# Seven block products for the third chunk's gate and up, with the pair's operand sums moved ahead, in an fp32 feed-forward kernel

## What is computed

```python
# first layer; every sequence b has its own low-rank matrices (rank 16), F = 1376
gate = x @ W_gate.T + 0.5 * lora(x, A_gate[b], B_gate[b])
up   = x @ W_up.T   + 0.5 * lora(x, A_up[b], B_up[b])
act  = silu(gate) * up
down = act @ W_down.T + 0.5 * lora(act, A_down[b], B_down[b])
x = x + down @ sign(W_ffn).T + bias0
# second layer
y = lora(x, B1[b], A1[b])
x = x + y @ (W1 + 2 * sum_n w_n * lora_B_n @ lora_A_n).T + bias1
```

## Time and profile before

| | us |
|---|---|
| median of 3 runs | 877.64 |
| lowest, highest | 876.82, 879.19 |
| the profiled execution | 876.61 |
| its span | 874.8 |

### The profile page before, as it was taken

One profiled execution on the slowest core, in us unless ns is written; L12 is line 12 of the kernel. 1 busy time (PEld: TensorE's weight loads), 2 busy tenths in 40 slices (PEclk: granted clock), 3 DMA queues, 4 the chain that ended last, 5 costly groups with the idle time before them and its releaser, 6 DMA issues.

```text
span 874.8 us, 21938 instructions
## 1 busy us (share of the span) xinstructions
PE 868.2 (99%) x7474; PEld 714.5 (82%) x7474; DVE 523.5 (60%) x1204; ACT 230.8 (26%) x460; POOL 86.5 (10%) x122
## 2 busy tenths in 40 slices
PE   9999999999999999999999999999999999999998
PEld 6888888888888888888888888888888888888885
DVE  5797555656555565656556655655656565556644
ACT  4953221222222122222212222212123122212210
POOL 0232000000000000000000000000000000000011
PEclk9999999999999999999999999999999999999999
DMA  9957777575777767577776757677775757777653
GB/s 338 415 218 251 237 232 249 188 242 156 235 248 227 244 209 238 156 234 231 236 236 226 241 166 233 195 248 239 230 243 176 235 175 243 246 226 247 204 133 94
DMA packets 161819, 197.22 MB, mean 225 GB/s; under 512 B 58112, under 2 KB 127744, under 8 KB 154112
## 3 DMA queue, kind: packets, MB, share of 16 engines
q1 hardware_dynamic: 103584, 108.76, 40.4%
q10 hardware_dynamic: 56096, 80.76, 27.3%
q0 software_dynamic: 2112, 7.34, 2.1%
HBM read 150.37 MB, written 15.20 MB: 189 GB/s over the span
## 4 chain that ended last, share of the span: by engine, by line
PE 95%; SPq 2%; DMA 1%; DVE 1%; issue 0%; ACT 0%; ACTq 0%; DVEq 0%
PE gu_ps L1132 54%; PE y_ps L1237 26%; PE out_ps L1259 3%; PE gu_ps L1346 2%; PE out_ps L1310 2%; PE gu_ps L1337 1%; PE y_ps L1132 1%; PE out_ps L1246 1%; PE out_ps L1132 1%; PE gu_ps L1237 1%; PE out_ps L1267 1%; DMA rows_sb<-in_btab 1%; SPq L352 0%; SPq L444 0%; DMA la_raw<-in_la 0%
## 5 line engine op out<-in xcount | busy, mean ns | idle before, releaser
L1237 PE MATMUL y_ps<-down_sb,actT_sb 128*128 128x512 f32 x1023 | 246.9, 394 | 0.0
L1237 PEld LDWEIGHTS y_ps<-down_sb,actT_sb 128*128 128x128 f32 x1023 | 189.7, 188 | 58.7 <-issue 21.4
L1132 PE MATMUL gu_ps<-wg_sb,xT_sb 128*128 128x432 f32 x768 | 163.8, 362 | 0.5 <-DVE act_all L842 0.5
L1132 PE MATMUL gu_ps<-wu_sb,xT_sb 128*128 128x432 f32 x768 | 160.7, 358 | 0.0
L1132 PEld LDWEIGHTS gu_ps<-wg_sb,xT_sb 128*128 128x128 f32 x768 | 141.7, 188 | 11.6 <-DVE xT_sb L824 1.4
L1132 PEld LDWEIGHTS gu_ps<-wu_sb,xT_sb 128*128 128x128 f32 x768 | 144.4, 188 | 8.0
L544 POOL TENSOR_TENSOR b_two<-b_raw,const_sb 128x128 f32<-128x128 f32 x62 | 23.5, 400 | 630.2 <-DMA b_raw<-in_b1tab 630.2
L598 ACT CAST actT_sb<-landed 128x512 fp32r<-128x512 f32 (+1 forms) x96 | 50.5, 584 | 127.1 <-issue 76.7
L610 ACT ACTIVATE act_all<-gu_ps 128x432 f32<-128x432 f32 (+1 forms) x96 | 49.6, 551 | 88.6 <-PE gu_ps L1337 83.6
L1132 PE MATMUL gu_ps<-slot,s_sb 128*128 128x512 f32 x270 | 66.8, 392 | 0.0
L846 DVE STREAM_TRANSPOSE act_all<-act_all 128x512 f32<-128x512 f32 (+1 forms) x96 | 64.0, 667 | 3.3
(11 more groups left out here) (173 smaller groups left out, 911.6 us busy)
## 6 DMA issues: line engine op xcount, KB each, us to landing
slot<-t_table ACTq DMA_DIRECT2D x59, 1024.0 KB, 7.7
a_raw<-in_atab SPq DMA_DIRECT2D x128, 152.0 KB, 7.5
rows_sb<-in_btab SPq DMA_DIRECT2D x128, 118.0 KB
landed<-act_all SPq DMA_DIRECT2D x132, 64.0 KB, 2.5
xT_raw<-in_xT SPq DMA_DIRECT2D x32, 256.0 KB, 6.3
x_in<-in_x SPq DMA_DIRECT2D x32, 256.0 KB, 8.1
landed<-act_all ACTq DMA_DIRECT2D x124, 64.0 KB, 2.7
out_x<-out_sb SPq DMA_DIRECT2D x31, 256.0 KB, 5.2
```

The costliest lines, as they stand in the source:

```text
L1132: last = nc.tensor.matmul(o, w, m, start=start and n == 0, stop=stop and n == len(terms) - 1, skip_group_check=not check)
L1237: last = nc.tensor.matmul(to[:], actT_sb[:, ACTT_SLOT[c] + n, a, :], down_sb[:, blk, b, :], start=begin and (c, n) == (0, 0) and (a, b) == ...
```

## The change

Chunk 2 gets the same seven block products (q1 to q7) as chunk 1. Its weights leave wg_sb and wu_sb and are kept as four blocks v11, v21, v12, v22; its differences of weights are made by GpSimd in the opening and stored unsplit in vt_table; in the loop ScalarE loads them (432 KB each, four times a pair) into vslot0 and vslot1, and they are split there each time (high_side_t, low_side_t). The products of a step are ordered anew, chunk 0 last. first_sums, low_s and high_s of the next pair go ahead of add_out, silu and gating in an odd step. x1_turn lies over x_in; the last step's x has a tile of its own. In the odd steps, send_act of chunk 1 and ScalarE's half of send_x1 move into the next even step. The core of the diff:

```diff
@@ SP, before step 0
+            sp.dma_start(vt_raw[1][:], wside[:, half(0)]).then_inc(S["vraw_in"], 16)
...
@@ GpSimd
             t_store(1, S["first_out"])
+            pool.wait_ge(S["vraw_in"], 4 * 16)
+            side_difference(1, 3, 1)
...
+            for n in range(1, 5):
+                pool.dma_start(vt_table[n - 1], vt_raw[n][:].rearrange("p k w -> p (k w)")).then_inc(S["vt_out"], 16)
             t_store(2, S["first_out"])
@@ ScalarE, step
                 if parity == 0 and seven(j):
-                    copy_p1(g, j)
+                    copy_p1(j)
+                    copy_q1(j)
+                    send_act(act, prev, 1)
+                    high_s(4, j)
+                    load_side_t(3)
+                    send_x1(act, pp, range(0, 2))
+                if isinstance(g, int) and g == 1:
+                    act.wait_ge(S["vt_out"], 4 * 16)
...
                 copy_lhs(g)
                 if parity == 0 and seven(j):
+                    load_t(3, L["slot0_in"])
                     load_t(4, L["slot1_in"])
-                    load_t(3, L["slot0_in"])
+                    high_side_t(3, j)
+                    high_side_t(4, j)
                 if parity == 1 and nxt is not None:
...
+                    load_side_t(1)
+                    load_side_t(2)
                     load_t(1, L["slot0_in"])
                     if seven(j):
                         load_t(2, L["slot1_in"])
...
+                if parity == 1 and nxt is not None:
+                    high_s(1, j + 1)
+                    high_s(2, j + 1)
+                for c in range(NC):
+                    silu(g, c)
+                if parity == 1 and nxt is not None:
+                    high_side_t(1, j + 1)
+                    high_side_t(2, j + 1)
@@ VectorE
             def even_products(g, j, prev):
...
+                add_block("u2", j, u2_sb[:], u2_sb[:], gu_ps[4][:], "p6", None)
+                add_block("u4", j, u4_sb[:], u2_sb[:], gu_ps[1][:], "p5", nth(SEVEN_SUM, "u2", j))
+                low_s(4, j)
...
+                add_block("v4", j, v4_sb[:], v2_sb[:], gu_ps[3][:, 0:SIDE], "q5", nth(SEVEN_SUM, "v2", j))
                 low_s(3, j)
+                split_actT(prev, 0)
+                add_block("up_even", j, gu_ps[1][:], u2_sb[:], gu_ps[1][:], "p3", None)
...
+            def odd_products(g, j, prev):
+                add_block("up_odd", j, gu_ps[1][:], u4_sb[:], gu_ps[0][:], "p7", nth(SEVEN_SUM, "u4", j))
+                add_block("vup_odd", j, gu_ps[3][:, 0:SIDE], v4_sb[:], gu_ps[2][:, 0:SIDE], "q7", nth(SEVEN_SUM, "v4", j))
...
@@ VectorE, step
+                if parity == 0 and seven(j):
+                    low_side_t(3, j)
+                    low_side_t(4, j)
+                if parity == 1 and nxt is not None:
+                    first_sums(j + 1)
                 if nxt is not None:
                     split_xT(nxt, 1 - parity)
+                if parity == 1 and nxt is not None:
+                    low_s(1, j + 1)
+                    low_s(2, j + 1)
                 if pp is not None:
                     after(dve, L["stored"], 16 * pp)
                     add_out(pp)
@@
                     gated(g, c)
                     turn_act(g, c)
                 if parity == 1 and nxt is not None:
-                    first_sums(j + 1)
-                    low_s(1, j + 1)
-                    low_s(2, j + 1)
+                    low_side_t(1, j + 1)
+                    low_side_t(2, j + 1)
@@ TensorE: even_blocks makes p1, q1, p5, q5, p6, q6, p2, q2, p3, q3
+                pe.wait_ge(L["act_done"], g * NC - NC + 2)
+                one(0, x_of(0), w11_sb, L["seven_mm"], True)
...
+                summed("v4", j)
+                one(3, s_of(0), v22_sb, L["seven_mm"], False, SIDE)
@@ TensorE: odd_blocks makes p7, q7, p4, q4
+                summed("up_odd", j)
                 slot_ready(1, 2 * j - 1)
+                one(0, x_of(1), slot1, L["seven_mm"], False)
@@ TensorE, step
                 elif parity == 0:
-                    p1(g, j)
-                    p6(g, j)
-                    p5(g, j)
-                    up(g, 0)
-                    p2(g, j)
-                    p3(g, j)
+                    even_blocks(g, j)
                     small_ready(g, prev, pp)
                     small(parity, prev, pp)
...
+                    first_gate(g)
+                    summed("v2", j)
+                    first_up(g, L["xT_used"])
                 else:
-                    p7(g, j)
-                    up(g, 0)
-                    p4(g, j)
+                    odd_blocks(g, j)
+                    first_gate(g)
                     small_ready(g, prev, pp)
                     small(parity, prev, pp)
-                gate(g, 2)
-                up(g, 2)
+                    first_up(g, L["xT_used"])
```

## The result

| | before | after |
|---|---|---|
| median, us | 877.8 | 904.85 |
| lowest, highest (4 runs each) | 876.82, 879.19 | 899.02, 908.94 |
| the profiled execution | 876.6 | 905.7 |
| its span | 874.8 | 903.6 |
| start of step 2 | 99.58 | 109.65 |

The ratio is 1.030, with an interval of 1.024 to 1.036.

What follows compares the result with a forecast made beforehand. TensorE, busy 99% of the span, was taken to bound the kernel. Against 876.6 us, -17.6 + 3 + 1.5 + 7.3 = -5.8 gives 870.8; with the median 1.0 higher, 871.8 us, whole range 862 to 889.

Steps and rivals of the forecast that it cites:

- Products: In each pair of steps chunk 2's gate and up take 42 matmuls instead of 48: 17.6 us less in 15 pairs.
- the p4 term: In odd steps TensorE's product p4 waits for up_odd, which VectorE starts only after turn_x1: 0.1 us x 15, 1.5 us.
- Rival 4: TensorE does not take less for the 42 products, since the new order adds gaps; chance included in Rival 3's.
- S: The end of TensorE's small products; in the odd step the next step was forecast to start at S + 11.97.
- The cover at the end of an odd step: The xT tile has 4.7 us to land; taken as 4.9, so 0.2 us in a pair, 3 us in 15.
- rival 1: In odd steps the xT wait, with first_sums ahead of gating, takes the gain back: 888 to 899 us; chance 0.23.
- rule of whole packets: An engine drains about 9 to 17 descriptors from one ring before turning; by it the xT wait's 3 us would be 0.
- The opening: Side sums and side stores on GpSimd ahead of T2 move step 2's start from 99.58 to 107: 7.3 us, once.
- Rival 2: The opening hides its own work, step 2 starts within 3 us of today, no xT wait: 864 us; chance 0.14.
- Rival 3: VectorE becomes the bound in even steps; one more collision with GpSimd opens 0.6 us there: 881 us; chance 0.10.

Runs made afterwards that it cites:

- side_load_behind: The changed kernel with only the 432 KB side load moved behind send_x1 on ScalarE in even steps, high_s(4) still first: 885.0 us.
- xT_behind_gathers: x1_and_t2_first with SyncE issuing the x^T tile behind the four gathers of atab in odd steps, some 2.5 us later: 1003.5 us.
- x1_sent_first: The changed kernel with ScalarE's half of send_x1 issued ahead of high_s(4) and of the side load in even steps: 884.3 us.
- x1_and_t2_first: The changed kernel with the edits of both x1_sent_first and t2_stored_first: 876.2 us.
- t2_stored_first: The changed kernel with T2's store put ahead of the side differences and side stores on GpSimd in the opening: 892.8 us.
- sums_behind_gating: x1_and_t2_first with sums s1 and s2 made and split behind the odd step's gating, ScalarE's copies behind its activations: 866.8 us.
- loads_behind_xT: x1_and_t2_first with ScalarE issuing its four table loads in odd steps only once the x^T tile has landed: 885.9 us.

## Why the prediction was wrong, point by point

**Products: right.** A pair without waits is 50.43 - 49.36 = 1.07 us shorter, where 1.17 less 0.1 (the p4 term) was forecast. The odd step is 20.94 us. Rival 4 falls.

**The move of ScalarE's x1 quarters: the step that failed.** The forecast's part on the change costs no line of it. It lists what moves on VectorE and what is loaded, but send_x1 went into the next even step behind send_act, s4's copy and load_side_t(3), and its landing is waited for at S. With 3.1 us to land it is hidden (side_load_behind); behind the 432 KB it took 4.4 and 5.1. Price: 17.8 us of waits, and 1.7 of clock at the longest of them. Without this one error the kernel would have come out at 884, inside the range, though still slower. None of the rivals named it.

**The cover at the end of an odd step: the law right, the landing right only in the loop.** Three numbers of it held: 4.7 us of room, paid once a pair beyond it (7.5 worked out, 7.66 seen in xT_behind_gathers), no wait in the loop, against 0.2 us forecast. From landing to the next step's start the forecast had 4.99 us; at the end of step 5 it was 4.91 in the changed kernel, in x1_sent_first, side_load_behind and x1_and_t2_first. The reason given for the landing was half wrong. I let rows of transfers mix by their sizes; what decided was what had been issued first. The side loads' two issues take 0.83 us of ScalarE's queue, so the slot loads go out at 417.15 instead of right at 416.3, and x^T slips in ahead of them. That margin is 0.84 us there and 0.4 in other pairs; that it exists was not foreseen, so the landing of about 4 us in the loop is in part luck. In steps 3 and 5, where SyncE came late from load_b (3.85 us for its last four issues in step 3), it was gone: rival 1 came true in two places of 15, for 8.0 us. The forecast worked out the Trainium skill's rule of whole packets (DMA: Bandwidth & Descriptors, "Queues, rings and completion order") to a landing well inside 4.7 us. It left out the packets that the tile has to wait for: 17 descriptors, the upper end of what the page calls typical, if each is a row of 8 KB, are 2.2 MB on 16 engines, 5.5 us at 406 GB/s as an estimate. With the 2.7 us of a tile that has nothing ahead of it that allows 8.2. The 6.3 to 8.1 us behind one slot load are compatible with it; the 8.7 to 10.2 behind all four loads would take longer packets.

**The opening: the size near by luck, the path wrong; 7.3 forecast, 10.1 measured.** The chain on which the 7.3 rest came about nearly as forecast: T2 at 92.23 against 89.5, T4 at 103.71 against 102, the gating that TensorE needs done at 107.69 against 107. The side differences took 9.56 us, where 8.1 and some growth to 10 were forecast, and began 1.7 us later. But this chain did not end last. TensorE's own path, put at 105.5, took until 109.65: two waits, 2.83 and 4.25 us, and some 3.3 us of lower clock with them. The first comes from VectorE's splits beside GpSimd's side differences, the second from the slow landing of act_all; neither is a term of the forecast. t2_stored_first shows the first: there VectorE's split of x^T takes 0.69 us and the wait is 0.52, as before the change. That the stores slowed act_all's landing is argued from the time at which they ran, not tested. Rival 2 falls. 5.6 us of the 10.1 hung on one position in GpSimd's queue (t2_stored_first).

**The clock: missing from the sum.** Each wait was priced at its own length. Where waits of some 4 us come, the matmuls behind them run at the lower level for 3.4 to 6.8 us: 1.7 us for the wait of 3.97 in x1_and_t2_first, 6.8 us in the loop of the changed kernel, some 3.3 in its opening.

**Rival 3 (VectorE against GpSimd): the collision is there, its price in the loop isn't.** s4's first sum takes 1.14 us in place of 0.43 in most even steps (median 1.13), in sums_behind_gating too (1.18 us), and no wait follows from it there. The view of the chain led through this sum all the same, because the queue behind it was late; side_load_behind takes it off the path. In the opening the same collision has a price that no rival named: the wait of 2.83 us.

## What to carry to other kernels

- List every DMA issue that a change moves, and for each what goes out ahead of it, in its own queue and in the others. A small transfer that somebody waits for belongs ahead of a large one that nobody needs yet: exchanging two lines was worth 20 us here.
- When parts of a change are undone one by one, compare the waits of each run before adding up the gains: here the same two waits, 8 us, went away in two different runs, and one of them in three more.
- Work placed ahead of a wait that others share should be work that the next reader needs. The sums were needed 2.5 us into the next step and were put ahead of the gating, which was needed at its start.
- A cover that depends on which of two engines issues first is as thin as the time between the issues. Read that distance in several steps, the early ones too, not in one.

## What the runs showed of the hardware

- Landing of a 256 KB tile in one queue, by what was issued before it in another: 2.4 to 4.1 us behind nothing, 3.5 to 4.7 behind 432 KB, 4.0 to 6.1 behind twice that, 7.4 to 9.0 with 1 MB more, 8.7 to 10.2 with 2 MB more. It grows with the bytes ahead, at about the rate of the stretch (406 GB/s).
- A 64 KB transfer: 2.0 to 2.4 us in the kernel before, 4.0 to 6.6 behind a 432 KB load in its own queue, 4.1 issued 0.37 us ahead of such a load in another queue.
- The granted clock at a wait of about 4 us: 0.50 for 6.8 us at one of 4.20, for 3.4 us at one of 3.79, and at two of 3.97 once for 3.4 (x1_and_t2_first) and once for 6.8 (side_load_behind); 0.63 in the mean over the 8.1 us behind one of 7.66. In the changed kernel's loop it stayed at 1.00 at 14 waits of 0.5 to 2.1 us and fell at one of 2.26. x1_and_t2_first, with one long wait, spread over 11.8 us in four runs (870.4 to 882.1), sums_behind_gating over 1.2; loads_behind_xT, whose longest wait is 2.3 us, spread over 11.9. What makes the spread stays open; the profiles show one execution each.
- A VectorE sum of 128 x 256 out of two tiles in SBUF takes 0.43 us alone and 1.14 to 1.18 while GpSimd adds the bias. A split of 128 x 512 takes 0.69 us alone and 2.49 beside GpSimd's subtractions.
